# Head attention on one Trainium2 core: the row maxima of an item taken bank by bank, with each bank released by itself

## The chip, the cores and the metric

The kernel runs on one core of a Trainium2 chip, with its five engines: TensorE (PE, with its weight loads shown apart as PEld), VectorE (DVE), ScalarE (ACT), GpSimd (POOL) and SyncE (SP, whose DMA queue is SPq). The metric is the device time of one execution in microseconds, as the median of several.

## The reference

The input x has 4 batches of 1024 tokens and 256 features. It is normalised, and two branches are added to it: a causal attention with one head, and a feed-forward block that begins with an attention of 16 heads. The change touches that attention alone.

```python
xn = _layernorm(x, axis=-1)
x = x + _L0_attn_ref(xn, L0_attn_W) + _L0_ffn_ref(xn, ...)
...
q = (src @ Wq).reshape(Bb, Tt, H, DH).transpose(0, 2, 1, 3)        # H = 16 heads of DH = 16
k = (src @ Wk_c @ Wk).reshape(Bb, Tt, H, DH).transpose(0, 2, 1, 3)
v = (src @ Wv_c @ Wv).reshape(Bb, Tt, H, DH).transpose(0, 2, 1, 3)
q = _apply_rope(q, sin, cos)
k = _apply_rope(k, sin, cos)
attn = jnp.einsum('bhqd,bhkd->bhqk', q, k) / np.sqrt(DH).astype(np.float32)
attn = jax.nn.softmax(attn, axis=-1)
sa = jnp.einsum('bhqk,bhkd->bhqd', attn, v)
```

## The kernel before

The program has stages, one behind the other: projections, the causal attention, the head attention (function `head_attention`, about 347 to 1085 us of the span), and the feed-forward. Only the head attention is changed.

It works in 16 steps (`STEPS`): one step is one batch with 4 heads (`GH`). Every score is computed twice. First come the scores with the queries on the partitions, of which only the row maxima are kept; the maxima are then put into two extra rows of q, so that the second product, with the keys on the partitions, has them subtracted already and goes straight to the exponential.

The first product is cut into 32 items a step (`ITEMS`), 512 in all. An item is 128 queries against 512 keys for two heads, the two *sides* (`SIDES` = 2). The side with g = 0 lies on partitions 0 to 63 and the one with g = 1 on 64 to 127, so one item is two matmuls on different row groups of TensorE. Each writes its own PSUM bank: `sq[slot % 2][:, g, :]`. There are two such double banks, and the items take them in turn. VectorE reduces the item to two maxima per partition (`maximum`, L1124, tile `h_halfmax`), and its end releases the double bank through `sq_free[slot % 2]`. TensorE's `item` (L1026) waits for that release of two items earlier; `sq_made` tells VectorE that an item is there. Once a step, `larger` (L1131) merges the half maxima, `turn_maxima` (L1034) transposes them through TensorE into the same double banks, and VectorE splits them into a rounded part and its rest (L1140, L1145); SyncE then writes these into q (`shift`).

The second product, the *k pair* (`score`, L1047, tile `h_sk`), gives two of the four heads of a *unit* (16 units a step, 256 in all) in two of three banks that take turns, and waits until ScalarE has emptied them. ScalarE's four exponentials of a unit (`fill`, L1094, tile `h_p`) each release one bank. `mix` (L1060, tile `h_po`) multiplies the probabilities with v.

The order on TensorE is written by hand. A unit is: first k pair, two items of maxima for a later step, second k pair, mix of the unit before. The maxima run ahead: 32 items of step 0, and 8 of step 1, come before the first unit. In the middle of a step a unit also holds the transposition. Each engine works through its own list in order, and a waiting instruction holds what stands behind it.

Of the kernel before, what the change touches and what calls it, by code (L numbers as in the profile page):

```python
# [8 lines left out]
ALU = mybir.AluOpType  # L9
AX = mybir.AxisListType  # L10

P = 128
B, S, D = 4, 1024, 256
N = B * S
CH = 512
# [26 lines left out]
SIDES = 2  # L42
# [814 lines left out]
def head_attention(nc, inputs, ot_d, ffw, first_chunk):  # L857
# [3 lines left out]
    with ExitStack() as ctx:  # L861
# [16 lines left out]
        TILES = GH * QT  # L878
        inputs.add_set(nc, ctx)
        q6, k6, vh = inputs.q6, inputs.k6, inputs.vh  # L880
        probs = [sb(f"h_p{i}", [P, GH, CH]) for i in range(PR)]
        outT = [sb(f"h_o{i}", [P, CH]) for i in range(NQ)]
        ident = sb("h_ident", [P, P])
        halfmax = [sb(f"h_halfmax{i}", [P, ITEMS, SIDES]) for i in range(2)]
        negm = sb("h_negm", [P, TILES])
# [22 lines left out]
        sq_made = sem("h_sq_made")  # L908
# [27 lines left out]
        with nc.Block() as block:  # L936
# [39 lines left out]
            @block.sync  # L976
            def _(sp):
                wait = Waits(sp, passed)

                def load(n):  # L980
                    r = n % RING
                    if n >= RING:
                        wait.ge(pv_done, (n - RING + 1) * UNITS)
                    else:
                        wait.ge(ones_set, SIDES)
                    inputs.load(sp, n, loaded[r])
                    if n > AHEAD:
                        wait.ge(spread, n - AHEAD)
                    inputs.load_values(sp, n, values_in)

                def shift(n):

                    r, slot = n % RING, turn_slot(n)
                    wait.ge(sq_free[slot % 2], slot // 2 + 1)
                    for g in range(SIDES):
                        for j in range(SHIFT):
                            row = g * SIDE_AT + DOTS + j
                            sp.dma_start(q6[r][row:row + 1, :, :].rearrange("o p t -> o (p t)").bitcast(F32),
                                         mparts[g * PAIRS * QT:(g + 1) * PAIRS * QT, j, :].bitcast(F32))\
                                .then_inc(shifted[r], 16)  # L1000

                load(AHEAD)
                shift(0)
                for n in range(STEPS):
                    if n == STEPS - 2:
                        for c in range(NQ):
                            sp.wait_ge(stored[c], (n - 1) * 16)
                        first_chunk.load_values(sp, 0, chunk_in)
                        first_chunk.load_xn(sp, 0, chunk_in)
                    if n and n + AHEAD < STEPS:  # L1010
                        load(n + AHEAD)
                    if n + 1 < STEPS:
                        shift(n + 1)

            @block.tensor
            def _(pe):
                def item(n, m):

                    p, i, half = m // (QT * NQ), m // NQ % QT, m % NQ
                    r, slot = n % RING, item_slot(n, m)  # L1020
                    if m == 0 and n >= AHEAD:
                        pe.wait_ge(loaded[r], loads_of(n) if n % RING >= AHEAD else loads_of(n) - LOADS * 16)
                    pe.wait_ge(sq_free[slot % 2], slot // 2)
                    for g in range(SIDES):
                        at = slice(g * SIDE_AT, g * SIDE_AT + DOTS)
                        ins = nc.tensor.matmul(sq[slot % 2][:, g, :], q6[r][at, p, i * P:(i + 1) * P],  # L1026
                                               k6[r][at, p, half * CH:(half + 1) * CH], start=True, stop=True)
                    ins.then_inc(sq_made, 1)

                def turn_maxima(n):  # L1030
                    slot = turn_slot(n)
                    pe.wait_ge(max_done, n + 1)
                    pe.wait_ge(sq_free[slot % 2], slot // 2)
                    nc.tensor.transpose(sq[slot % 2][0:TILES, 0, 0:P], negm[:, :], ident[:, :]).then_inc(sq_made, 1)  # L1034

                def score(n, w, p):

                    c, j = divmod(w, QT)
                    r, f = n % RING, n * FILLS + w * GH + p * SIDES
                    if w == 0 and p == 0:  # L1040
                        pe.wait_ge(shifted[r], shifts_of(n))
                    emptied = [before[f + g] for g in range(SIDES) if before[f + g] is not None]
                    if emptied:
                        pe.wait_ge(exp_done, max(emptied) + 1)
                    for g in range(SIDES):
                        at = slice(g * SIDE_AT, g * SIDE_AT + ROWS)
                        ins = nc.tensor.matmul(spread_banks[bank_at(f + g)], k6[r][at, p, j * P:(j + 1) * P],  # L1047
                                               q6[r][at, p, c * CH:(c + 1) * CH], start=True, stop=True)
                    ins.then_inc(scored, 1)

                def mix(n, w):
                    c, j = divmod(w, QT)
                    u = n * UNITS + w
                    if j == 0:
                        pe.wait_ge(out_taken, n * NQ + c)
                    if w == 0 and n >= AHEAD:
                        pe.wait_ge(spread, n - AHEAD + 1)
                    pe.wait_ge(exp_done, (u + 1) * GH)
                    for h in range(GH):
                        ins = nc.tensor.matmul(po[h * VW:(h + 1) * VW, :], vh[n % RING][:, j, h, :],  # L1060
                                               probs[u % PR][:, h, :], start=j == 0, stop=j == QT - 1)
                    ins.then_inc(pv_done, 1)

                pe.wait_ge(const_set, 2)
                for m in range(ITEMS):
                    item(0, m)
                for m in range(HELD):
                    item(1, m)
                turn_maxima(0)
                for m in range(HELD, LEAD * PER):  # L1070
                    item(1, m)
                for u in range(STEPS * UNITS + 1):
                    n, w = divmod(u, UNITS)
                    ahead = [divmod(u * PER + ITEMS + LEAD * PER + b, ITEMS) for b in range(PER)]
                    if n < STEPS:
                        score(n, w, 0)
                    if ahead[0][1] == HELD and ahead[0][0] <= STEPS:
                        turn_maxima(ahead[0][0] - 1)
                    for coming in ahead:
                        if coming[0] < STEPS:  # L1080
                            item(*coming)
                    if n < STEPS:
                        score(n, w, 1)
                    if u:
                        mix(*divmod(u - 1, UNITS))
# [34 lines left out]
            def _(dve):  # L1120
                def maximum(n, m):
                    slot = item_slot(n, m)
                    dve.wait_ge(sq_made, slot + 1)
                    nc.vector.tensor_reduce(halfmax[n % 2][:, m, :], sq[slot % 2][:, :, :], AX.X, ALU.max)\  # L1124
                        .then_inc(sq_free[slot % 2], 1)

                def larger(n):

                    for last in (item_slot(n, ITEMS - 2), item_slot(n, ITEMS - 1)):
                        dve.wait_ge(sq_free[last % 2], last // 2 + 1)  # L1130
                    nc.vector.tensor_reduce(negm[:, :].rearrange("p (g t) -> p t g", g=SIDES),  # L1131
                                            halfmax[n % 2][:, :, :].rearrange("p (t a) g -> p t g a", a=NQ),
                                            AX.X, ALU.max, negate=True).then_inc(max_done, 1)

                def round_maxima(n):
                    slot = turn_slot(n)
                    dve.wait_ge(sq_made, slot + 1)
                    if n:
                        dve.wait_ge(shifted[(n - 1) % RING], shifts_of(n - 1))
                    nc.vector.tensor_copy(mparts[:, HI, :], sq[slot % 2][0:TILES, 0, 0:P]).then_inc(m_rounded, 1)  # L1140

                def rest_of_maxima(n):
                    slot = turn_slot(n)
                    dve.wait_ge(m_rounded, n + 1)
                    nc.vector.tensor_tensor(mparts[:, LO, :], sq[slot % 2][0:TILES, 0, 0:P],  # L1145
                                            mparts[:, HI, :].bitcast(F32), ALU.subtract)\
                        .then_inc(sq_free[slot % 2], 1)

                for n in range(STEPS + 1):
                    for m in range(ITEMS):  # L1150
# [613 lines left out]
```

## Time and profile before

| | |
|---|---|
| time before, median of 3 runs | 1753.97 us (1751.2 to 1754.52) |
| the profiled execution's own time | 1746.94 us |
| its span, first to last instruction | 1745.2 us |
| TensorE / weight loads / VectorE / ScalarE / GpSimd busy | 1567.1 / 934.7 / 1152.7 / 854.4 / 265.7 us |
| mean granted TensorE clock | 0.965 of full speed |
| the reductions of L1124: 512 | 601.2 us busy, 1218 ns each |

The span leaves out 1.7 us around the profiled execution. Busy times of different engines overlap, so they don't add up to the span. Matmuls are pipelined: one row of two matmuls that lasts 0.50 us doesn't mean that TensorE could start the next only 0.50 us later.

### The profile page before, as it was taken

What the parts mean: (1) busy time and instruction counts of PE and PEld (TensorE: products, weight loads), DVE (VectorE), ACT (ScalarE), POOL (GpSimd) and SP (SyncE); (2) the same over time, 40 slices, a digit from 0 to 9 for tenths busy, and PEclk for the clock granted to TensorE, in tenths of its full rate; (3) what the DMA queues carried; (4) which work ended last, traced back from release to release, by engine and by line L of the source; (5) the groups of instructions that cost most, each with busy time, mean ns of one, the idle gap of its engine ahead of it and who ended that gap; (6) DMA issues with size and microseconds to landing.
All of it is one profiled execution on the core that took longest, in us unless ns stands there. A gap on an engine that the chain in (4) does not pass through costs nothing. (4 is left out here: it accounts for less than half of the span.)

```text
span 1745.2 us, 22955 instructions
## 1 busy us (share of the span) xinstructions
PE 1567.1 (90%) x8336; PEld 934.7 (54%) x8336; DVE 1152.7 (66%) x1612; ACT 854.4 (49%) x1572; POOL 265.7 (15%) x226
## 2 busy tenths in 40 slices
PE   7887948769999999999999987899999999999997
PEld 4554736523333333333333322688888888888886
DVE  3776625498888888888888880455564637465543
ACT  2444313207888888888888887412132222223130
POOL 1224910144210000000000000302020212112020
PEclk9999979958999999999999999899999999999999
DMA  5789673151433333333333311210101101010000
GB/s 193 260 277 354 176 166 120 37 96 56 92 68 56 56 56 56 56 56 56 56 56 56 60 45 34 58 37 12 50 24 36 48 12 60 0 60 0 25 1 25
DMA packets 95827, 132.73 MB, mean 76 GB/s; under 512 B 22896, under 2 KB 65792, under 8 KB 95744
## 3 DMA queue, kind: packets, MB, share of 16 engines
q1 hardware_dynamic: 85392, 107.51, 24.9%
q0 software_dynamic: 4496, 14.70, 3.3%
q10 hardware_dynamic: 5856, 9.44, 1.8%
q8 instruction: 50, 0.82, 0.2%
q14 instruction: 33, 0.27, 0.1%
HBM read 76.56 MB, written 54.53 MB: 75 GB/s over the span
## 5 line engine op out<-in xcount | busy, mean ns | idle before, releaser
L1124 DVE TENSOR_REDUCE h_halfmax<-h_sq 128x2 f32<-128x1024 f32 x512 | 601.2, 1218 | 79.0 <-PE h_sq L1026 78.9
L1094 ACT ACTIVATE h_p<-h_sk 128x512 f32<-128x512 f32 x988 | 538.7, 598 | 177.9 <-PE h_sk L1047 157.5
L1411 PE MATMUL f_ob<-w_experts,f_h 128*128 128x512 f32 x1536 | 364.6, 396 | 0.0
L1411 PEld LDWEIGHTS f_ob<-w_experts,f_h 128*128 128x128 f32 x1536 | 287.7, 188 | 66.9
L1047 PE MATMUL h_sk<-h_q,h_k 50*128 50x512 f32 x988 | 247.3, 494 | 56.8 <-ACT h_p L1094 56.0
L1060 PE MATMUL h_po<-h_p,h_v 128*32 128x512 f32 x2048 | 274.3, 608 | 6.1 <-ACT h_p L1094 3.6
L1047 PEld LDWEIGHTS h_sk<-h_q,h_k 50*128 50x128 f32 x988 | 93.3, 184 | 337.0 <-ACT h_p L1094 324.4
L1026 PE MATMUL h_sq<-h_k,h_q 48*128 48x512 f32 x1024 | 196.3, 450 | 25.6 <-DVE h_halfmax L1124 14.2
L1026 PEld LDWEIGHTS h_sq<-h_k,h_q 48*128 48x128 f32 x1024 | 100.9, 194 | 97.5 <-DVE h_halfmax L1124 75.4
L1637 DVE SCALAR_TENSOR_TENSOR h_spare<-f_ob,f_wt,h_spare 128x256 f32<-128x256 f32 x128 | 61.8, 483 | 127.1 <-PE f_ob L1411 123.8
L1296 POOL TENSOR_TENSOR f_h<-h_spare,f_h 128x512 fp32r<-128x512 f32 x64 | 82.3, 1292 | 348.0 <-ACT f_h L1467 348.0
L1623 DVE TENSOR_TENSOR h_spare<-h_spare,f_pair 128x512 f32<-128x512 f32 x64 | 44.0, 688 | 96.4 <-ACT h_spare L1474 95.9
L1392 PE MATMUL f_pair<-f_x1p,w_routed 128*128 128x512 f32 x384 | 94.2, 404 | 0.2
L1392 PE MATMUL f_pair<-f_x1p,w_shared 128*128 128x512 f32 x384 | 90.6, 395 | 0.0
L727 PE MATMUL a_out<-a_v,a_pT 128*128 128x256 f32 x432 | 64.4, 301 | 28.4 <-DVE a_pT L792 28.4
L955 POOL COPY h_v<-h_values 128x512 f32<-128x512 f32 x14 | 8.6, 612 | 513.4 <-DMA h_values<-vh_d 513.4
L1474 ACT ACTIVATE h_spare<-f_pair 128x512 f32<-128x512 f32 x64 | 38.3, 598 | 97.5 <-PE f_pair L1392 96.9
L1392 PEld LDWEIGHTS f_pair<-f_x1p,w_routed 128*128 128x128 f32 x384 | 73.2, 193 | 18.0 <-DVE h_spare L1623 1.5
L1392 PEld LDWEIGHTS f_pair<-f_x1p,w_shared 128*128 128x128 f32 x384 | 72.3, 188 | 16.9
L1060 PEld LDWEIGHTS h_po<-h_p,h_v 128*32 128x32 f32 x2048 | 40.4, 108 | 75.7 <-ACT h_p L1094 50.0
L701 PE MATMUL a_sc<-c_kT,c_qT 128*128 128x512 f32 (+3 forms) x192 | 70.6, 507 | 7.2 <-POOL a_mask L646 7.2
L727 PEld LDWEIGHTS a_out<-a_v,a_pT 128*128 128x128 f32 x432 | 56.4, 196 | 36.0 <-DVE a_pT L792 22.4
(166 smaller groups left out, 1471.7 us busy)
## 6 DMA issues: line engine op xcount, KB each, us to landing
h_q<-q_d SPq DMA_DIRECT2D x84, 128.0 KB, 6.1
h_k<-k_d SPq DMA_DIRECT2D x84, 128.0 KB, 7.1
ot_d<-h_o ACTq DMA_DIRECT2D x32, 256.0 KB, 3.8
q_d<-t_parts SPq DMA_DIRECT2D x12, 512.0 KB, 5.0
k_d<-t_parts SPq DMA_DIRECT2D x12, 512.0 KB, 5.2
p_xin<-in_L_attn_x SPq DMA_DIRECT2D x8, 512.0 KB, 5.2
xn_d<-p_xn SPq DMA_DIRECT2D x8, 512.0 KB, 3.7
xnT_d<-p_xnT SPq DMA_DIRECT2D x8, 512.0 KB, 5.8
```

What stands on the lines that cost most here:

```text
L701: ins = nc.tensor.matmul(sc[u % 2][:, c:c + w], qT[s][:, k, i * P:(i + 1) * P], kT[s][:, k, c:c + w], start=k == 0, stop=k == KD - 1)
L727: ins = nc.tensor.matmul(out[u % 2][:, 0:D], pT[u % 2][left][:, j, :], vp[s][right][:, j, :], start=j == 0 and n == 0, stop=j == i and n = ...
L1026: ins = nc.tensor.matmul(sq[slot % 2][:, g, :], q6[r][at, p, i * P:(i + 1) * P], k6[r][at, p, half * CH:(half + 1) * CH], start=True, stop ...
L1047: ins = nc.tensor.matmul(spread_banks[bank_at(f + g)], k6[r][at, p, j * P:(j + 1) * P], q6[r][at, p, c * CH:(c + 1) * CH], start=True, sto ...
L1060: ins = nc.tensor.matmul(po[h * VW:(h + 1) * VW, :], vh[n % RING][:, j, h, :], probs[u % PR][:, h, :], start=j == 0, stop=j == QT - 1)
L1094: nc.scalar.activation(probs[u % PR][:, h, :], spread_banks[bank_at(f)], ACT.Exp, scale=DH ** -0.5).then_inc(exp_done, 1)
L1124: nc.vector.tensor_reduce(halfmax[n % 2][:, m, :], sq[slot % 2][:, :, :], AX.X, ALU.max)\
L1296: nc.gpsimd.tensor_tensor(h[LO][:, f, :], whole[f % 2], h[HI][:, f, :].bitcast(F32), ALU.subtract).then_inc(h_split, 1)
L1392: ins = nc.tensor.matmul(ps[:, half, :], w[a][:, k, at:at + P], x1p[b][:, k, :], start=n == 0, stop=n == len(terms) - 1)
L1411: ins = nc.tensor.matmul(to, h[left][:, KH * shared + k, at], weight, start=n == 0, stop=n == len(terms) - 1)
L1623: nc.vector.tensor_tensor(whole[f % 2], sil[f % 2], pair[p][:, 1, :], ALU.mult)\
L1637: link(nc.vector.scalar_tensor_tensor(x1[s][:, j, :], ob[b][:, 0:D], wt[s][:, j, 2 * g:2 * g + 1], x1[s][:, j, :], ALU.mult, ALU.add))
```

## The change

The reduction of an item over both banks becomes two reductions over one bank each. TensorE now signals each matmul by itself, VectorE waits for each by itself, each reduction releases its own bank, and TensorE waits before each matmul for the release of that one bank. `sq_free` and `sq_made` so count banks where they counted items. The transposed maxima, which take one bank of a double bank, count for both.

```diff
-                    wait.ge(sq_free[slot % 2], slot // 2 + 1)
+                    wait.ge(sq_free[slot % 2], (slot // 2 + 1) * SIDES)
...
-                    pe.wait_ge(sq_free[slot % 2], slot // 2)
                     for g in range(SIDES):
                         at = slice(g * SIDE_AT, g * SIDE_AT + DOTS)
-                        ins = nc.tensor.matmul(sq[slot % 2][:, g, :], q6[r][at, p, i * P:(i + 1) * P],
-                                               k6[r][at, p, half * CH:(half + 1) * CH], start=True, stop=True)
-                    ins.then_inc(sq_made, 1)
+                        if slot >= 2:
+                            pe.wait_ge(sq_free[slot % 2], (slot // 2 - 1) * SIDES + g + 1)
+                        nc.tensor.matmul(sq[slot % 2][:, g, :], q6[r][at, p, i * P:(i + 1) * P],
+                                         k6[r][at, p, half * CH:(half + 1) * CH], start=True, stop=True)\
+                            .then_inc(sq_made, 1)
...
                 def turn_maxima(n):
                     slot = turn_slot(n)
                     pe.wait_ge(max_done, n + 1)
-                    pe.wait_ge(sq_free[slot % 2], slot // 2)
-                    nc.tensor.transpose(sq[slot % 2][0:TILES, 0, 0:P], negm[:, :], ident[:, :]).then_inc(sq_made, 1)
+                    pe.wait_ge(sq_free[slot % 2], slot // 2 * SIDES)
+                    nc.tensor.transpose(sq[slot % 2][0:TILES, 0, 0:P], negm[:, :], ident[:, :]).then_inc(sq_made, SIDES)
...
                 def maximum(n, m):
                     slot = item_slot(n, m)
-                    dve.wait_ge(sq_made, slot + 1)
-                    nc.vector.tensor_reduce(halfmax[n % 2][:, m, :], sq[slot % 2][:, :, :], AX.X, ALU.max)\
-                        .then_inc(sq_free[slot % 2], 1)
+                    for g in range(SIDES):
+                        dve.wait_ge(sq_made, slot * SIDES + g + 1)
+                        nc.vector.tensor_reduce(halfmax[n % 2][:, m, g:g + 1], sq[slot % 2][:, g, :], AX.X, ALU.max)\
+                            .then_inc(sq_free[slot % 2], 1)
...
-                        dve.wait_ge(sq_free[last % 2], last // 2 + 1)
+                        dve.wait_ge(sq_free[last % 2], (last // 2 + 1) * SIDES)
...
-                    dve.wait_ge(sq_made, slot + 1)
+                    dve.wait_ge(sq_made, (slot + 1) * SIDES)
...
-                        .then_inc(sq_free[slot % 2], 1)
+                        .then_inc(sq_free[slot % 2], SIDES)
```

On VectorE, at the start of the head attention, the list before is this (`p_made10` is the semaphore `sq_made` under the name of an earlier stage whose place it took, `p_made20` and `p_made11` are the two of `sq_free`):

```order
L1124 TENSOR_REDUCE h_halfmax<-h_sq 128x2 [waits p_made10] x32
L1131 TENSOR_REDUCE h_negm<-h_halfmax 128x16x2 [waits p_made20,p_made11]
L1124 TENSOR_REDUCE h_halfmax<-h_sq 128x2 [waits p_made10] x2
L1140 CAST h_mparts<-h_sq 32x128 [waits p_made10]
L1145 TENSOR_TENSOR h_mparts<-h_sq,h_mparts 32x128 [waits p_made30]
```

After the change the same place reads as follows.

```order
L1126 TENSOR_REDUCE h_halfmax<-h_sq 128x1 [waits p_made10] x64
L1133 TENSOR_REDUCE h_negm<-h_halfmax 128x16x2 [waits p_made20,p_made11]
L1126 TENSOR_REDUCE h_halfmax<-h_sq 128x1 [waits p_made10] x4
L1142 CAST h_mparts<-h_sq 32x128 [waits p_made10]
L1147 TENSOR_TENSOR h_mparts<-h_sq,h_mparts 32x128 [waits p_made30]
```

Nothing has changed its place; each reduction has become two of half the length, with a wait each.

On TensorE, a unit in the middle of the stage is this before (`p_var_done1` is `exp_done`, ScalarE's count of exponentials):

```order
L1047 MATMUL h_sk<-h_q_50,h_k_52 128x512 [waits p_var_done1]
L1047 MATMUL h_sk<-h_q_50,h_k_52 128x512
L1026 MATMUL h_sq<-h_k,h_q 128x512 [waits p_made11]
L1026 MATMUL h_sq<-h_k,h_q 128x512
L1026 MATMUL h_sq<-h_k,h_q 128x512 [waits p_made20]
L1026 MATMUL h_sq<-h_k,h_q 128x512
L1047 MATMUL h_sk<-h_q_50,h_k_52 128x512 [waits p_var_done1]
```

A unit after the change, with the two items in the middle again, is this:

```order
L1048 MATMUL h_sk<-h_q_50,h_k_52 128x512 [waits p_var_done1]
L1048 MATMUL h_sk<-h_q_50,h_k_52 128x512
L1027 MATMUL h_sq<-h_k,h_q 128x512 [waits p_made11] x2
L1027 MATMUL h_sq<-h_k,h_q 128x512 [waits p_made20] x2
L1048 MATMUL h_sk<-h_q_50,h_k_52 128x512 [waits p_var_done1]
```

The order is the same, but all four matmuls of the two items now wait, where one of each two did.

## Rows read from the trace of the kernel before

**Rows 1.** The page: the group of the reductions (busy us, mean ns | idle before, releaser)

```profile
L1124 DVE TENSOR_REDUCE h_halfmax<-h_sq 128x2 f32<-128x1024 f32 x512 | 601.2, 1218 | 79.0 <-PE h_sq L1026 78.9
```

**Rows 2.** Windows of the stage: busy us by engine, granted clock, DMA share, GB/s

```profile
core 0: us, PE busy (x) PEld busy (x) DVE busy (x) ACT busy (x) POOL busy (x), PEclk, DMA share, GB/s
347.30:394.80 47.50, 32.62 (x85) 12.03 (x85) 46.11 (x44) 0.93 (x2) 22.42 (x22) 0.50 0.53 95
394.80:404.60 9.80, 9.04 (x36) 3.14 (x36) 6.99 (x7) 5.58 (x11) 4.84 (x4) 0.50 0.27 60
404.60:1083.80 679.20, 611.64 (x3995) 203.98 (x3991) 566.93 (x513) 559.97 (x1044) 35.59 (x33) 1.00 0.33 57
```

**Rows 3.** Timeline of one unit: start us, us, work, [idle before, releaser]

```profile
600.02 0.50 PE L1047 MATMUL h_sk<-h_q,h_k 50*128 50x512 f32 x2
...
600.35 0.68 PE L1026 MATMUL h_sq<-h_k,h_q 48*128 48x512 f32 x4
600.53 0.18 PEld L1026 LDWEIGHTS h_sq<-h_k,h_q 48*128 48x128 f32 x2 [0.21 <-DVE h_halfmax L1124]
600.62 2.28 ACT L1094 ACTIVATE h_p<-h_sk 128x512 f32<-128x512 f32 x4 [0.40 <-PE h_sk L1047]
600.78 2.36 DVE L1124 TENSOR_REDUCE h_halfmax<-h_sq 128x2 f32<-128x1024 f32 x2 [0.31 <-PE h_sq L1026]
...
601.26 0.50 PE L1047 MATMUL h_sk<-h_q,h_k 50*128 50x512 f32 x2 [0.23 <-ACT h_p L1094]
...
601.69 1.07 PE L1060 MATMUL h_po<-h_p,h_v 128*32 128x512 f32 x8
...
602.69 0.50 PE L1047 MATMUL h_sk<-h_q,h_k 50*128 50x512 f32 x2
...
603.19 0.19 PEld L1026 LDWEIGHTS h_sq<-h_k,h_q 48*128 48x128 f32 x2 [0.21 <-DVE h_halfmax L1124]
```

**Rows 4.** Timeline of the next unit's start, and of its second k pair

```profile
603.29 2.28 ACT L1094 ACTIVATE h_p<-h_sk 128x512 f32<-128x512 f32 x4 [0.40 <-PE h_sk L1047]
603.46 2.36 DVE L1124 TENSOR_REDUCE h_halfmax<-h_sq 128x2 f32<-128x1024 f32 x2
603.94 0.19 PEld L1047 LDWEIGHTS h_sk<-h_q,h_k 50*128 50x128 f32 x2 [0.56 <-ACT h_p L1094]
```

**Rows 5.** Timeline of the unit with the transposition

```profile
606.12 0.28 DVE L1140 CAST h_mparts<-h_sq 32x128 fp32r<-32x128 f32 x1 [0.30 <-PE h_sq L1034]
...
606.77 0.50 PE L1026 MATMUL h_sq<-h_k,h_q 48*128 48x512 f32 x2 [0.26 <-DVE h_mparts L1145]
```

**Rows 6.** Waits of the weight loads, 404 to 1030 us (total us, times, longest)

```profile
PEld h_sk L1047 <- ACT h_p L1094: 305.0, 434, 1.5
PEld h_sq L1026 <- DVE h_halfmax L1124: 41.1, 187, 0.3
```

**Rows 7.** Timeline of VectorE, and of TensorE's last item, before the first unit's second k pair

```profile
348.15 36.29 DVE L1124 TENSOR_REDUCE h_halfmax<-h_sq 128x2 f32<-128x1024 f32 x32 [8.19 <-PE h_sq L1026]
384.70 2.35 DVE L1124 TENSOR_REDUCE h_halfmax<-h_sq 128x2 f32<-128x1024 f32 x2
...
387.93 9.14 DVE L1124 TENSOR_REDUCE h_halfmax<-h_sq 128x2 f32<-128x1024 f32 x8 [0.39 <-PE h_sq L1026]
...
394.87 0.79 PE L1026 MATMUL h_sq<-h_k,h_q 48*128 48x512 f32 x2 [0.34 <-DVE h_halfmax L1124]
```

**Rows 8.** The reductions of the causal stage by form (busy us, mean ns)

```profile
L765 DVE TENSOR_REDUCE a_negm<-a_sc 128x1 f32<-128x1024 f32 x4 | 4.9, 1225 | 0.1
L765 DVE TENSOR_REDUCE a_negm<-a_sc 128x1 f32<-128x512 f32 x4 | 2.8, 691 | 0.1
```

**Rows 9.** Timeline of ScalarE in the first units

```profile
393.87 1.08 ACT L1094 ACTIVATE h_p<-h_sk 128x512 f32<-128x512 f32 x2 [56.97 <-PE h_sk L1047]
...
405.42 0.60 ACT L1094 ACTIVATE h_p<-h_sk 128x512 f32<-128x512 f32 x1 [1.08 <-PE h_sk L1047]
```

## The prediction, made before the changed kernel was run

> **What bounds the kernel now.** The windows of the stage come first [rows 2]. From 404.6 to 1083.8 us TensorE is busy for 90% of the time, VectorE for 83%, ScalarE for 82%. With three engines that close together shares decide nothing, so the next view is the timeline of one unit [rows 3]. Its repeat is 603.29 - 600.62 = 2.67 us, from ScalarE's first exponential of one unit to that of the next [rows 3, 4]. The reader is to follow what releases what round this ring. The exponential starts at 600.62; its end releases the second k pair at 601.26; the mix stands behind that at 601.69; the next unit's first k pair stands behind the mix at 602.69; the exponential follows at 603.29. The steps are 0.64, 0.43, 1.00 and 0.60 us and make 2.67 us. VectorE is in none of them. It works off its two items in 2.36 us and idles 0.31 us, waiting for TensorE.
>
> TensorE does wait for VectorE in this unit: 0.21 us before the weights of the second item [rows 3], and 41.1 us in total over the stage [rows 6]. But the k pair behind that item then idles 0.23 us for ScalarE [rows 3], so what the item gains by coming earlier, the k pair loses again waiting. I read the 41.1 us as off the path.
>
> Before the units it is different. From 347.3 to 394.8 us VectorE is busy 46.11 of 47.5 us [rows 2]: 32 reductions without a gap, 2 more, the turn of the maxima, and 8 more [rows 7]. TensorE's last item before the first unit's second k pair waits for VectorE (394.87) [rows 7], so the whole stage starts later by whatever this stretch loses. 32 + 2 + 6 = 40 reductions end before that wait is over.
>
> **The price of a reduction of half the length.** The trace has it: 1024 elements take 1225 ns, 512 take 691 ns, both from PSUM, in the causal stage [rows 8]. What counts is the distance from start to start. The 32 reductions in a row last 36.29 us, so that distance is (36.29 - 1.22) / 31 = 1.131 us, 0.087 us under their mean duration of 1.218 us [rows 1, 7]: neighbours overlap. No row here shows two short ones in a row with that wait. The bounds are 1.131 / 2 = 0.566 us (a second instruction costs nothing) and 0.691 us (no overlap). I take the same overlap, 0.691 - 0.087 = 0.604 us, since it's what this very instruction has behind a fulfilled wait. An item then costs VectorE 2 x 0.604 = 1.208 us, 0.077 us more than before.
>
> The Trainium skill prices it otherwise: its page "VectorE: DVE Perf Modes", section "The TRN2 errata — SBUF-src ops pay a fixed extra latency per instruction", gives an operation from PSUM 120 cycles plus one per element at 0.96 GHz, and warns against many small tiles. By that table, an estimate, an item goes from 1.192 to 1.317 us, 0.125 us more, and the sum below would be about +4.6 us where it is +2.7. The rows agree with neither figure exactly, and they decide.
>
> **The sum.**
> 1. The stretch before the units: 40 items x 0.077 = +3.1 us, all of it on the path. (Bounds: 40 x 0 and 40 x 0.251 = +10.0 us.)
> 2. In that stretch VectorE idles 0.39 us behind the turn of the maxima, since the item after it could start only when both banks were free [rows 7]. Its first bank is now free 0.6 us earlier, so its first reduction can follow the rest of the maxima at once: -0.4 us.
> 3. A normal unit: 0. VectorE's first reduction starts as before, since both matmuls of the first item find their banks free and still run side by side. The four reductions last 3 x 0.604 + 0.691 = 2.50 us where the two lasted 2.36, so they end 0.14 us later, 0.17 us before the next unit's first item arrives (600.78 + 2.50 = 603.28 against 603.46 [rows 3, 4]). The last bank is released 0.14 us later, so the last matmul of the second item loads its weights at 603.33 instead of 603.19. Before, 0.50 us after that load the matmuls were over at the latest (0.50 us is the row of such a pair that had to load first, 606.77 [rows 5]). That gives 603.83, and the second k pair behind waits for ScalarE until 603.94 [rows 4]. The cover is 0.11 us. If it is gone, each further 0.01 us costs up to 2.4 us over some 240 units.
> 4. The matmuls of the second item no longer run side by side: the first finds its bank free 0.6 us sooner, the second waits. That too is held in the same cover.
> 5. The added waits and signals: one more wait per item on TensorE, none between instructions that are late today; the signal rides on the matmul. 0, bounded above by the cover of point 3.
> 6. The unit with the transposition, 15 times: the cast starts at 606.12 [rows 5]. VectorE would end its four reductions, begun at 603.46, at 605.96: still in time, with 0.16 us left. The second item there waits for the split of the maxima, which doesn't move. 0.
>
> Sum: 3.1 - 0.4 = +2.7 us, on the profiled execution from 1746.9 to 1749.6 us. The profiled execution lies 7 us under the median of the runs; on that median of 1753.97 the sum gives 1756.7 us, 0.15% more.
>
> **The rivals.**
> - *The last matmul pushes the ring* (chance 0.12). Everything in points 3 to 5 rests on 0.11 us of cover. Two matmuls that run one behind the other rather than side by side, with an own load and an own wait, may need more. For it: before, TensorE's pair of items took 0.68 us together. Against: the k pair had 0.23 us of idle time. If a unit grows by 0.04 us, 240 x 0.04 + 2.7 = about +12 us, 1766 us. It decides from 0.004 us over the cover.
> - *Short reductions do not overlap* (0.05). By the section "The DRAIN you can't avoid" of the page "VectorE: DVE Perf Modes" of the Trainium skill the next operation starts only when the pipe is empty; the trace disagrees for the long ones, which overlap by 0.087 us. The mechanism in rows: at 0.691 us each, four need 2.76 us, 0.09 us over the ring, and VectorE becomes the bound: 240 x 0.09 + 10.0 - 0.4 = +31 us, 1785 us. It decides from 2.67 / 4 = 0.668 us.
> - *A price between the two* (0.10): a reduction that costs 0.63 to 0.66 us in a row keeps the units and adds 40 x (0.13 to 0.19) = +5 to +7.5 us to the stretch before them, 1759 to 1761 us.
> - *TensorE's clock rises sooner* (0.08). Through the whole first stretch and the first three units the granted clock is half, 1.2 GHz [rows 2]. Those three units take 405.42 - 393.87 = 11.55 us [rows 9] where three at full clock take 8.0. With the matmuls of an item one behind the other TensorE is occupied for a larger share of the stretch, and the clock might rise before it ends: -3.5 + 2.7 = -0.8 us, 1753 us. Against: nothing in the rows says what it takes.
> - *The wait for VectorE was on the path* (0.05, the other side). If the second item's earlier first matmul brings the k pair forward, up to the 41.1 us of [rows 6] come back: 1716 us at best. Against: the 0.23 us of waiting for ScalarE behind it, and a ring that adds up without VectorE.
>
> **How the numbers follow.** What a measurement of this kernel can tell from no change is about 0.2%, 3.5 us. The forecast (0.60) at +2.7 us lies just inside: I give it 0.45 for no difference that can be told and 0.15 for slower. The clock case adds 0.06 to the same and 0.02 to faster; the pushed ring, the missing overlap and the middling price add 0.27 to slower; the other side adds 0.05 to faster. So faster has 0.07, the same 0.51 and slower 0.42. The likeliest case's own range is 1754 to 1760 us. The range for 8 in 10 takes in the clock case below and the pushed ring above, and leaves out the missing overlap and the other side: 1752 to 1766 us.
>
> **What would show it.** In the changed kernel's profile the short reductions should last 691 ns and stand 0.60 us apart, their group some 640 us busy (601.2 + 512 x 0.077). The first stretch should be longer by 2.7 us. The ring should stay at 2.67 us, with TensorE's k pair still idle for ScalarE. TensorE's item matmuls should no longer wait 0.21 us as a pair; only the last one should. VectorE's idle time in a unit should fall from 0.31 to 0.17 us. I'm wrong if the ring changes, above all if the k pair's idle time for ScalarE is gone, or if the reductions stand more than 0.63 us apart.

## The result, and the profile after

| | before | after |
|---|---|---|
| median of 20 runs | 1754.53 us (1751.2 to 1759.23) | 1757.44 us (1753.43 to 1762.04) |
| span of the profiled execution | 1745.2 us | 1754.4 us |
| reductions of the maxima | 512 | 1024 |

The changed kernel takes 1.0021 times as long, with a 95% interval of 1.0013 to 1.0028: +3.7 us, between 2.3 and 4.9 (the two medians of the table lie 2.9 us apart; the ratio is the better measure). The forecast was +2.7 us, 0.15%. The spans differ by 9.2 us, but 5.6 us of that are there before the head attention begins (its first reduction starts at 348.15 and at 353.74 us), and 1.1 us behind its last exponential, in code that is the same. So the comparison is made inside the stage.

The page of the changed kernel has this group for that of [rows 1] (busy us, mean ns | idle before, releaser):

```profile
L1126 DVE TENSOR_REDUCE h_halfmax<-h_sq 128x1 f32<-128x512 f32 x1024 | 633.9, 683 | 51.2 <-PE h_sq L1027 49.8
```

The waits of the weight loads from 410 to 1036 us have this for the second row of [rows 6] (total us, times, longest):

```profile
PEld h_sq L1027 <- DVE h_halfmax L1126: 3.0, 15, 0.2
```

VectorE's group grows from 601.2 to 633.9 us, and TensorE's wait for it has nearly gone: from 41.1 us [rows 6] to 3.0. That wait was no cost. The unit in the timeline of the changed kernel shows why (start us, us, work, [idle before, releaser]), to be held against [rows 3, 4]:

```profile
607.55 0.80 PE L1027 MATMUL h_sq<-h_k,h_q 48*128 48x512 f32 x4
607.81 2.27 ACT L1095 ACTIVATE h_p<-h_sk 128x512 f32<-128x512 f32 x4 [0.40 <-PE h_sk L1048]
607.97 2.48 DVE L1126 TENSOR_REDUCE h_halfmax<-h_sq 128x1 f32<-128x512 f32 x4 [0.18 <-PE h_sq L1027]
608.46 0.19 PEld L1048 LDWEIGHTS h_sk<-h_q,h_k 50*128 50x128 f32 x2 [0.43 <-ACT h_p L1095]
...
610.49 2.27 ACT L1095 ACTIVATE h_p<-h_sk 128x512 f32<-128x512 f32 x4 [0.40 <-PE h_sk L1048]
```

The ring is 610.49 - 607.81 = 2.68 us as before. VectorE works 2.48 us and idles 0.18 where it worked 2.36 and idled 0.31. The items' matmuls end at 607.55 + 0.80 = 608.35, and the k pair's load, which waits for ScalarE, comes at 608.46: the cover of 0.11 us that the prediction gave is there to the hundredth. (The ends of matmuls are modelled in the profile, so the hundredth is not to be leaned on.)

Before the units VectorE has no idle time to give. Its timeline, against [rows 7]:

```profile
353.74 38.36 DVE L1126 TENSOR_REDUCE h_halfmax<-h_sq 128x1 f32<-128x512 f32 x64 [8.18 <-PE h_sq L1027]
392.21 0.22 DVE L1133 TENSOR_REDUCE h_negm<-h_halfmax 128x32 f32<-128x64 f32 x1
392.35 2.48 DVE L1126 TENSOR_REDUCE h_halfmax<-h_sq 128x1 f32<-128x512 f32 x4
394.74 0.27 DVE L1142 CAST h_mparts<-h_sq 32x128 fp32r<-32x128 f32 x1
395.11 0.28 DVE L1147 TENSOR_TENSOR h_mparts<-h_sq,h_mparts 32x128 fp32r<-32x128 f32 x1
395.32 9.04 DVE L1126 TENSOR_REDUCE h_halfmax<-h_sq 128x1 f32<-128x512 f32 x15
```

The 32 items take 38.36 us where they took 36.29: (38.36 - 0.68) / 63 = 0.598 us from start to start, 0.065 us more per item. The idle time of 0.39 us behind the turn is gone. ScalarE's first units, against [rows 9]:

```profile
401.48 1.09 ACT L1095 ACTIVATE h_p<-h_sk 128x512 f32<-128x512 f32 x2 [58.98 <-PE h_sk L1048]
403.87 1.09 ACT L1095 ACTIVATE h_p<-h_sk 128x512 f32<-128x512 f32 x2 [1.30 <-PE h_sk L1048]
405.35 1.09 ACT L1095 ACTIVATE h_p<-h_sk 128x512 f32<-128x512 f32 x2 [0.40 <-PE h_sk L1048]
```

The first exponential comes 401.48 - 353.74 = 47.74 us behind the first reduction; before it came 393.87 - 348.15 = 45.72 us behind it. That is +2.0 us. Of the 40 items of the prediction only 38 have to be reduced before it; the last two hold up the second k pair of the first unit. So the first unit is longer too: from 401.48 to 405.35 it takes 3.87 us, where the kernel before has 3.75 (393.87 to 397.62). That is another +0.1 us.

What the prediction did not have is in the unit with the transposition. In the kernel before, the subtraction behind the cast of [rows 5] is this:

```profile
606.43 0.28 DVE L1145 TENSOR_TENSOR h_mparts<-h_sq,h_mparts 32x128 fp32r<-32x128 f32 x1
```

In the changed kernel the same place is this:

```profile
613.32 0.28 DVE L1142 CAST h_mparts<-h_sq 32x128 fp32r<-32x128 f32 x1
613.70 0.28 DVE L1147 TENSOR_TENSOR h_mparts<-h_sq,h_mparts 32x128 fp32r<-32x128 f32 x1
...
614.03 0.50 PE L1027 MATMUL h_sq<-h_k,h_q 48*128 48x512 f32 x2 [0.30 <-DVE h_mparts L1147]
```

From the cast to the subtraction it is 0.38 us, where it was 606.43 - 606.12 = 0.31. TensorE's second item and the k pair behind it wait for that subtraction. Read from the starts of the units' first exponentials, 14 units take 3.13 us instead of 3.06, and nearly all others 2.68 as before. (Sixteen maxima are turned. The first turn comes before the units, and behind the last there is no item left, so that unit takes 2.67 us in both kernels: 14 and not 15, as the prediction has it.)

### The profile page after: what moved, and what is told of

Read it like the earlier page. It is cut to its first block and busy times, and to the rows that moved or that the text cites. A ratio compares the mean times of both kernels' runs of the same rounds, so it can differ in the third digit from the quotient of the medians.

```text
span 1754.4 us, 23482 instructions
## 1 busy us (share of the span) xinstructions
PE 1613.0 (92%) x8336; PEld 990.4 (56%) x8336; DVE 1185.6 (68%) x2124; ACT 854.7 (49%) x1572; POOL 265.6 (15%) x226
## 5 line engine op out<-in xcount | busy, mean ns | idle before, releaser
L1126 DVE TENSOR_REDUCE h_halfmax<-h_sq 128x1 f32<-128x512 f32 x1024 | 633.9, 683 | 51.2 <-PE h_sq L1027 49.8
L1027 PE MATMUL h_sq<-h_k,h_q 48*128 48x512 f32 x1024 | 237.1, 454 | 12.6 <-POOL h_ident L944 7.9
L1027 PEld LDWEIGHTS h_sq<-h_k,h_q 48*128 48x128 f32 x1024 | 152.1, 195 | 74.9 <-DVE h_halfmax L1126 28.1
```

Source lines behind the costliest of these rows:

```text
L1126: nc.vector.tensor_reduce(halfmax[n % 2][:, m, g:g + 1], sq[slot % 2][:, g, :], AX.X, ALU.max)\
```

## The experiments

In all of them *stretch* is the time from the first reduction to the first exponential, and *units* are the distances between the units' first exponentials. Ratios are to the kernel before, with 95% intervals. Differences of 1 to 3 us are at the edge of what the times tell, and the rows of the stage tell them to 0.1 us; so the rows carry most verdicts.

### 1. The transposition signals by 1

```diff
-                    nc.tensor.transpose(sq[slot % 2][0:TILES, 0, 0:P], negm[:, :], ident[:, :]).then_inc(sq_made, SIDES)
+                    nc.tensor.transpose(sq[slot % 2][0:TILES, 0, 0:P], negm[:, :], ident[:, :]).then_inc(sq_made, 1)
...
-                        .then_inc(sq_free[slot % 2], SIDES)
+                        .then_inc(sq_free[slot % 2], 1)
```

The waits on both semaphores take their values from a table of the signals that each slot gives.

> The changed kernel, but the transposed maxima signal the release of their double bank by 1 instead of by 2, and every wait counts accordingly. Theory: in the changed kernel the signal by 2 took the wait out of the subtraction (L1147) into an instruction of its own, 0.07 us later, and that lies on the path of the 15 units with a transposition (3.13 us instead of 3.06). Here the subtraction should carry its wait again, those units should take 3.06 us, all other units 2.67, and the head attention should be 1.0 us shorter than in the changed kernel; the time should be some +2 us over the kernel before. Rival: the 0.07 us come from the bank-wise release of the item ahead of the transposition; then the units stay at 3.13 us.

Stretch 47.7 us; units 2.68 and 3.06 us; ratio 1.0012 (1.0000 to 1.0024), +2.1 us. The same place in the timeline of this kernel:

```profile
613.38 0.28 DVE L1154 CAST h_mparts<-h_sq 32x128 fp32r<-32x128 f32 x1
613.69 0.28 DVE L1159 TENSOR_TENSOR h_mparts<-h_sq,h_mparts 32x128 fp32r<-32x128 f32 x1
```

The 0.31 us are back, and the bank-wise release is still there, so the rival falls. The stretch falls by 0.07 us too, from 47.74 to 47.67, since the first turn lies in it. The page counts 23482 instructions for the changed kernel and 23466 for this one, 16 fewer, and in the trace those 16 are waits of VectorE that stand alone ahead of the subtraction, one a step. A subtraction that signals by 1 carries its wait itself; here, with a signal by 2, it did not. Once in the stretch and in 14 units, 15 x 0.07 = 1.0 us is the price.

### 2 and 3. Half reductions only ahead of the units, or only in them

```diff
+        parts = {turn_slot(n): 1 for n in range(STEPS)}
+        parts.update({item_slot(n, m): SIDES if n * ITEMS + m < ITEMS + LEAD * PER else 1 ...})
...
+                    if parts[slot] == 1:
+                        dve.wait_ge(sq_made, made_by(slot))
+                        nc.vector.tensor_reduce(halfmax[n % 2][:, m, :], sq[slot % 2][:, :, :], AX.X, ALU.max)\
+                            .then_inc(sq_free[slot % 2], 1)
+                        return
```

Experiment 3 has the two values the other way round. The transposition signals by 1 in both.

> Half reductions with bank-wise release only for the 40 items ahead of the first unit, whole ones behind; the transposition signals by 1. Theory: all that is left of the change's cost is in this stretch: from the first reduction to the first exponential 47.7 us as in the changed kernel, 2.0 us over the kernel before (40 x 0.065 less 0.4 to 0.6 behind the turn of the maxima), units as before, time about +2 us over the kernel before. Rival (the cost is spread over the units): stretch of 45.7 us and no difference in time.

> The other way round: whole reductions for the first 40 items, half ones with bank-wise release in all units; the transposition signals by 1. Theory: stretch to the first exponential 45.7 us, units 2.67 and 3.06 us, time that of the kernel before within 0.5 us, though VectorE gets 472 instructions more. Rival (the last matmul of an item pushes the ring, or the added instructions cost in the units): units over 2.68 us, +2 us or more.

With the halves first the stretch is 47.7 us and the units are 2.68 and 3.06; ratio 1.0018 (1.0007 to 1.0028). With the halves later the stretch is 45.7 us and the units are the same; ratio 1.0008 (0.9994 to 1.0023). The rows put the 2.0 us in the stretch and 0.1 us in the first unit (3.88 us with the halves first, 3.75 with them later), and nothing in the 236 units whose items are reduced in halves. The times agree but, with intervals that overlap, would not show it alone. VectorE's rows with the halves later, in the last items ahead of the units and in the first unit:

```profile
387.97 6.88 DVE L1133 TENSOR_REDUCE h_halfmax<-h_sq 128x2 f32<-128x1024 f32 x6 [0.42 <-PE h_sq L1034]
394.77 2.47 DVE L1138 TENSOR_REDUCE h_halfmax<-h_sq 128x1 f32<-128x512 f32 x4
```

### 4. The signals and waits alone

Whole reductions (the table above with 1 everywhere), but TensorE signals and waits for each matmul.

> Whole reductions as in the kernel before, one release for both banks, but TensorE signals each matmul by itself and waits before each: the added signals and waits without the added reductions. Theory: they cost nothing, stretch 45.7 us, units 2.67 and 3.06 us, time of the kernel before within 0.5 us. Rival (each added wait costs 0.05 us in TensorE's sequencer and the two matmuls of an item no longer run side by side): units of 2.7 us or more, +8 us or more.

Stretch 45.7 us, units 2.68 and 3.06; ratio 0.9991 (0.9978 to 1.0004). The added waits and signals cost nothing.

### 5. The cut alone

```diff
-                    nc.vector.tensor_reduce(halfmax[n % 2][:, m, :], sq[slot % 2][:, :, :], AX.X, ALU.max)\
-                        .then_inc(sq_free[slot % 2], 1)
+                    for g in range(SIDES):
+                        ins = nc.vector.tensor_reduce(halfmax[n % 2][:, m, g:g + 1], sq[slot % 2][:, g, :], AX.X,
+                                                      ALU.max)
+                    ins.then_inc(sq_free[slot % 2], 1)
```

> The kernel before with each reduction cut into two, but with one wait ahead of the two and one release behind them: the price of the cut without the bank-wise release. Theory: 40 x 0.065 = +2.6 us to the first exponential (48.3 us), since the idle time behind the turn of the maxima (0.39 us) stays; units 2.67 us and 3.06 us. Rival (the release by bank costs, not the cut): stretch of 45.7 us.

Stretch 405.25 - 357.09 = 48.16 us, units 2.68 and 3.06; ratio 1.0023 (1.0010 to 1.0035). VectorE's timeline:

```profile
357.09 38.36 DVE L1125 TENSOR_REDUCE h_halfmax<-h_sq 128x1 f32<-128x512 f32 x64 [8.19 <-PE h_sq L1026]
...
399.06 9.66 DVE L1125 TENSOR_REDUCE h_halfmax<-h_sq 128x1 f32<-128x512 f32 x16 [0.39 <-PE h_sq L1026]
```

The 64 take the same 38.36 us and the idle time of 0.39 us is back. The cut costs 48.16 - 45.72 = +2.4 us in the stretch, not the expected +2.6, because 38 items and not 40 lie ahead of the first exponential. The other two show in the first unit, 3.88 us instead of 3.75, so the cut costs 2.6 us in all. The release by bank gives back 48.16 - 47.74 = 0.4 us, or 0.5 against experiment 1, which doesn't pay the 0.07 us of the turn. Those are the two first terms of the sum, each by itself.

### 6. Quarters: how much cover do the units have?

```diff
+                        for c in range(2):
+                            ins = nc.vector.tensor_reduce(halfmax[n % 2][:, 2 * m + c, g:g + 1],
+                                                          sq[slot % 2][:, g, c * (CH // 2):(c + 1) * (CH // 2)],
+                                                          AX.X, ALU.max)
+                        ins.then_inc(sq_free[slot % 2], 1)
```

The tile of the half maxima doubles with it, so the merge once a step reads twice as much (0.29 us instead of 0.22).

> As the changed kernel with the transposition signalling by 1, but each bank is reduced in two pieces of 256 elements, the bank released behind the second. By the overlap measured (0.065 us more than the elements' time for each reduction) a piece stands 0.332 us from the next. Stretch to the first exponential: 40 x (4 x 0.332 - 1.131) = +7.9 us less 0.5. In the units the eight pieces take 2.66 us of 2.67 and the last bank is released 0.24 us later than in the changed kernel. By the cover that the prediction gave (0.11 us at the changed kernel's release, used up here) the second k pair comes 0.13 us late and a unit takes 2.80 us: +30 us more. The rival theory, that a late matmul needs only its load and its stream ahead of the k pair and not its whole recorded 0.50 us, has units of 2.67 to 2.70 us: together +8 to +15 us.

Stretch 52.6 us, +6.9; ratio 1.0089 (1.0065 to 1.0113), +15.6 us. A normal unit still takes 2.68 us, one with the transposition 3.42 on average. One unit of this kernel:

```profile
617.93 0.50 PE L1055 MATMUL h_sk<-h_q,h_k 50*128 50x512 f32 x2
...
618.81 0.18 PEld L1034 LDWEIGHTS h_sq<-h_k,h_q 48*128 48x128 f32 x1 [0.36 <-DVE h_halfmax L1139]
619.17 0.19 PEld L1055 LDWEIGHTS h_sk<-h_q,h_k 50*128 50x128 f32 x2 [0.18 <-ACT h_p L1102]
...
620.60 0.50 PE L1055 MATMUL h_sk<-h_q,h_k 50*128 50x512 f32 x2
```

The last matmul's weights are loaded only 0.36 us ahead of the k pair's, and the k pair waits for ScalarE all the same: the unit takes 620.60 - 617.93 = 2.67 us. So the expectation by the cover fell and its rival held, though its +8 to +15 us came out just short: where the prediction set aside 0.50 us for a late matmul, 0.36 are enough. What breaks first is the unit with the transposition: VectorE is still at its pieces and the longer merge when the transposition ends, and the cast starts 0.67 us behind the transposition's start where it was 0.32 before. That costs 14 x 0.36 = 5.0 us. With 0.4 us in the first unit it makes 6.9 + 0.4 + 5.0 = 12.3 us, inside the interval of the times (11.4 to 19.8).

### 7, 8 and 11. The two places of cost, used for a faster kernel

The maxima 3 units ahead instead of 4 (experiment 7), the second item of the transposition's unit behind the second k pair (11), and both (8), all with whole reductions:

```diff
-        LEAD = 4
+        LEAD = 3
...
+                    turning = ahead[0][1] == HELD and n < STEPS
+                    ahead = [coming for coming in ahead if coming[0] < STEPS]
+                    for coming in ahead[:1] if turning else ahead:
+                        item(*coming)
                     if n < STEPS:
                         score(n, w, 1)
+                    for coming in ahead[1:] if turning else []:
+                        item(*coming)
```

> The kernel before with the maxima 3 units ahead instead of 4 (LEAD = 3): two items fewer stand ahead of the first unit. Theory: that stretch is bound by VectorE and on the path, so its 38 instead of 40 reductions give back 2 x 1.131 = 2.3 us: 43.4 us to the first exponential or to the second k pair. What could cost: the shifted maxima land some 4 us behind the transposition, and two units behind it the first k pair of the next step waits for them; from the timeline they land at about 611 us and that pair comes at 611.1, so up to 0.5 us a step may be lost, 7 us. Rival (the stretch is not on the path): no gain at all.

> As the one with the maxima 3 units ahead, and in the unit with the transposition the second item stands behind the second k pair, so that this pair no longer waits for the split of the maxima. Theory: those units fall from 3.06 to about 2.90 us, 15 x 0.16 = 2.4 us less, on top of the 2.3 us; together -4.7 us against the kernel before, less what the landing of the maxima costs. Rival: the late item delays the mix by as much as the k pair gains, and the units stay at 3.06 us.

> The kernel before with whole reductions and the maxima 4 units ahead, and only the second item of the unit with the transposition put behind the second k pair. Theory: these 15 units take 2.90 instead of 3.06 us, everything else stays: -2.4 us, a ratio of 0.9986. Rival (what the k pair gains is lost at the mix, or later at VectorE): 3.06 us and a ratio of 1.000.

*Three units ahead*: the first exponential comes 1.6 us sooner and the second unit 2.3 us sooner, as expected of two items fewer on the path. But the time does not fall: ratio 1.0013 (1.0000 to 1.0025). The first k pair now waits for the maxima's transfer, 0.34 us in the first unit (the row below). By the trace the first k pairs of the last four steps come late for it as well, and the units ahead of them take 3.00, 2.76, 3.03 and 3.42 us instead of 2.68, 1.5 us together. That leaves 1.5 - 2.3 = -0.8 us by the rows. In this profile the clock rose only 15.7 us behind the first exponential, and three units took 4.13 us or more.

```profile
397.44 0.80 PE L1047 MATMUL h_sk<-h_q,h_k 50*128 50x512 f32 x2 [0.34 <-DMA h_q<-h_mparts]
```

*The late item*: 14 units take 2.91 us instead of 3.06. Alone, ratio 0.9992 (0.9979 to 1.0005); with the three units ahead, 1.0005 (0.9989 to 1.0020). In the timeline of experiment 11 the k pair no longer waits for the split:

```profile
607.90 2.27 ACT L1097 ACTIVATE h_p<-h_sk 128x512 f32<-128x512 f32 x4 [0.40 <-PE h_sk L1047]
...
608.55 0.50 PE L1047 MATMUL h_sk<-h_q,h_k 50*128 50x512 f32 x2
...
608.89 0.40 PE L1026 MATMUL h_sq<-h_k,h_q 48*128 48x512 f32 x2
...
610.82 2.28 ACT L1097 ACTIVATE h_p<-h_sk 128x512 f32<-128x512 f32 x4 [0.64 <-PE h_sk L1047]
```

The rows give 14 x 0.15 = 2.1 us, and the stage from the first reduction to the last exponential takes 730.0 us against 731.9. The ratio fits the 0.9986 that was expected, and fits no gain too.

By its rows the fastest kernel of the study is experiment 8, with both edits: 1.9 us less up to the second unit, 2.1 us less in the 14 units and 0.9 us lost to the transfer make -3.1 us. Its times don't show that gain: their interval begins at -1.9 us. The granted clock of the runs goes some way to say why. A run's time follows it: of the 29 runs of the kernel before beside experiments 7 and 8, the fastest (1746.99 us) had 0.965 and the slowest (1757.58 us) 0.959. On average these 29 had 0.9614, the 12 runs of each of the two experiments 0.9598; with the clock at half or full that is 2 x 0.0016 x 1754 = some 6 us more at 1.2 GHz. At 1 - 2.68 / 4.14 = 0.35 us for each, that is some +2 us (an estimate from the units' two lengths), and brings the sums from the rows of both experiments inside their intervals. Whether the kernels themselves bring the lower clock about stays open.

### 9 and 10. Both kernels once more

> The kernel before once more, to see what differs between two profiled executions of one program: I expect the stretch to the first exponential (45.7 us), the units (2.67 and 3.06 us) and the feed-forward to repeat within 0.1 us, and the start of the head attention and the moment at which TensorE's clock rises to move by several us.

> The changed kernel once more: stretch 47.7 us and units of 2.67 and 3.13 us again. Theory: the rise of the clock, 8.8 us behind the first exponential in the first profile of it, falls elsewhere here, for no reason in the program. Rival: it is tied to the changed order of the matmuls, and comes 8.8 us behind again where the kernel before has 10.7 us.

Stretches 45.7 and 47.7 us again; units 2.68 with 3.06 and 3.13 again. The first reduction started at 355.5 and 356.1 us, 7.3 and 2.3 us later than in the first profiles. TensorE's clock rose from 1.2 to 2.4 GHz 6.9 us (before) and 8.1 us (changed) behind the first exponential, where it had been 10.7 and 8.8: it moves farther between the two executions of the kernel before (3.8 us) than between the kernels (1.9 and 1.2 us), and over all 13 profiles from 6.6 to 17.0 us. Each unit ahead of it takes up to 4.14 us instead of 2.68. From the last exponential to the end of the program, mostly the feed-forward, it is 665.2 and 664.9 us (before), 666.3 and 665.1 us (changed), so the expected 0.1 us was missed, and the time of a single execution can't tell 1 us. And in the second profile of the changed kernel the clock fell once more for ten microseconds near the end of the units, where no items are left:

```profile
1040.00:1053.00 13.00, 11.08 (x69) 3.70 (x69) 9.78 (x16) 10.81 (x21) 0.00 (x0) 1.00 0.06 22
1053.00:1064.00 11.00, 9.79 (x38) 2.36 (x38) 5.64 (x2) 6.23 (x13) 0.00 (x0) 0.53 0.02 3
```

(The columns are those of [rows 2].) TensorE was busy for 85% of the window ahead, and for 89% of the one with the fall. The four units in it took 3.9 us more together. Of the other twelve profiles two have a fall within the units, of 3.4 us at 1073 us, in kernels with whole reductions (experiments 4 and 9), so the changed kernel has no claim to it.

## Why the prediction was right, point by point

- *What bounds the stage.* Right. The ring through ScalarE and TensorE stayed at 2.68 us while 38 us of TensorE's waiting for VectorE disappeared. The wait was off the path: the k pair behind it waits for ScalarE.
- *The price of a short reduction.* 0.604 us from start to start forecast, 0.598 measured. The overlap of 0.087 us was right (0.683 - 0.598 = 0.085). The duration was not: 691 ns came from the causal stage, where the long ones last 1225 ns and not the 1218 of this stage, and the short ones here last 683 ns. By the table of the Trainium skill's page "VectorE: DVE Perf Modes" (section "The TRN2 errata — SBUF-src ops pay a fixed extra latency per instruction"), an estimate, a reduction that is cut in two costs 0.125 us more; these rows have 0.065, and they decide. Its warning against small tiles holds here in kind, at half the size. The section "The DRAIN you can't avoid" of the same page of the Trainium skill says that the next operation doesn't start until the pipe is empty, and that one that is not held starts earlier. Here the short ones overlap like the long ones: 683 ns long, they stand 598 ns apart.
- *Point 1*, +3.1 us forecast, +2.6 measured (experiment 5: 2.4 to 2.5 in the stretch, 0.1 in the first unit). The cause is the 0.077 us per item that were 0.065.
- *Point 2*, -0.4 us forecast, -0.5 measured (experiment 5 against experiment 1).
- *Points 3 to 5*, 0 forecast, 0 measured (experiments 3 and 4); the cover was 0.11 us as worked out. It was also read too narrowly: experiment 6 used 0.25 us (a load 0.36 us ahead of the k pair where the changed kernel has 0.61) without a loss.
- *Point 6*, 0 forecast, +1.0 us measured. This is the step that failed. The prediction said that the second item "waits for the split of the maxima, which doesn't move". It moves by 0.07 us, because the signal by 2 sets the subtraction's wait apart (experiment 1). That is 1.0 us: 14 such units, not 15, and once more in the stretch. The order of VectorE's instructions, which lists a wait with its instruction either way, doesn't show it.
- *The sum*, +2.7 us forecast: 2.6 - 0.5 + 1.0 = +3.1 us or, from the stretch, the first unit and the 14 units directly, 2.0 + 0.1 + 0.9 = +3.0 us, and +3.7 (2.3 to 4.9) in the times. An error of -0.6 us in the first two points and one of +1.0 us in the last partly cancel; that the sum came so near is luck to that extent. The two profiles themselves have 2.5 us between them, from the first reduction to the last exponential (731.9 and 734.4 us), and not 3.1, because the clock rose earlier in that of the changed kernel: its third unit took 2.76 us where the other's took 3.66.
- *The rivals.* The pushed ring, the missing overlap and the price between the two all fell on the units' 2.68 us and the 0.598 us. The wait on the path fell on [rows 6] against the row of after. That the clock rises sooner with the matmuls one behind the other is not borne out: the two profiles of the changed kernel have 8.8 and 8.1 us, the two of the kernel before 10.7 and 6.9, and the 20 runs of the changed kernel had a mean granted clock of 0.9604 where the 35 of the kernel before beside experiments 1 to 4 had 0.9613. Its premise did come true. From 352.9 to 402.9 us, the stretch and a little more, TensorE was busy for 48.68 of 50 us where it was 32.62 of 47.5 before [rows 2], and the granted clock stayed at 0.50 all the same:

```profile
352.90:402.90 50.00, 48.68 (x88) 23.27 (x89) 48.94 (x84) 1.09 (x2) 23.10 (x22) 0.50 0.53 99
```

## What to carry to other kernels

A stall that a row shows (here 41 us in 187 waits) is worth nothing if the next instruction on that engine waits for someone else anyway: look at what the instruction behind it waits for before paying for its removal. In this kernel cutting an instruction in two was free where the engine had slack within the loop, and was paid in full where the engine ran without a gap, so price the cut on the prologue too. If an instruction both waits and signals on a path that counts, look whether a signal by more than 1 has split its wait off, as it did here.

## What was not expected of the hardware

- An instruction of VectorE with a wait and a signal by 1 carries both; with a signal by 2 its wait became an instruction of its own, and the instruction started 0.07 us later (0.38 instead of 0.31 us behind the cast). It was seen on the subtraction alone.
- A late matmul, on the other row group than its neighbour, needed no more than 0.36 us between the start of its weight load and the start of the next pair's (experiment 6), though the rows of such matmuls last 0.50 us.
- In the changed kernel TensorE was busy for 97% of the 50 us up to 402.9 us at a granted clock of 0.50, and the clock rose only at 410.3 us.
- TensorE's granted clock fell to 1.2 GHz from 1053 to 1064 us in one execution, behind a window in which it was busy for 85% of the time (experiment 10).
